# Cross-attention with a routed sign-weight FFN on one core: the gate as stationary operand in four column groups

## The reference

```python
router_logits = n @ gate_w.T                # 1024 tokens x 8 experts
routing = softmax(router_logits)
in_scale = routing @ in_channel_scale       # 1024 x 512
out_scale = routing @ out_channel_scale
out = n * in_scale @ sign(weight).T * out_scale + bias
x = x + out
```

## Time and profile before

| | |
|---|---|
| median of 3 runs | 800.81 us (800.28 to 801.17) |
| the profiled execution | 800.34 us, span 798.5 us |
| TensorE busy | 793.7 us, 99% of the span |
| VectorE, ScalarE, GpSimd busy | 636.6, 359.2, 296.7 us |

### The profile page before, as it was taken

One profiled execution on the slowest core, in us unless ns is written; L12 is line 12 of the kernel. 1 busy time (PEld: TensorE's weight loads), 2 busy tenths in 40 slices (PEclk: granted clock), 3 DMA queues, 4 the chain that ended last, 5 costly groups with the idle time before them and its releaser, 6 DMA issues.

```text
span 798.5 us, 12698 instructions
## 1 busy us (share of the span) xinstructions
PE 793.7 (99%) x4090; PEld 674.9 (85%) x4090; DVE 636.6 (80%) x1066; ACT 359.2 (45%) x949; POOL 296.7 (37%) x279
## 2 busy tenths in 40 slices
PE   9999999999999999999999999999999999999998
PEld 7888888888888888888888888888888888888886
DVE  6877878886893596888888788888888888877775
ACT  6633432432341253545444444444444444447683
POOL 3113021020111032736535544644564454435136
PEclk9999999999999999999999999999999999999999
DMA  8354774584466658627755766575566657553002
GB/s 301 146 196 174 224 247 138 175 266 161 154 191 205 206 166 275 207 65 226 236 163 163 239 191 205 163 240 171 175 210 202 204 157 240 162 196 141 1 1 106
DMA packets 103216, 145.53 MB, mean 182 GB/s; under 512 B 9944, under 2 KB 74584, under 8 KB 97648
## 3 DMA queue, kind: packets, MB, share of 16 engines
q1 hardware_dynamic: 102720, 144.33, 55.5%
q10 hardware_dynamic: 432, 0.39, 0.2%
HBM read 93.31 MB, written 51.38 MB: 181 GB/s over the span
## 4 chain that ended last, share of the span: by engine, by line
PE 98%; DMA 1%; DVE 0%; issue 0%; ACT 0%; SPq 0%; DVEq 0%
PE out L1455 11%; PE out L1457 11%; PE out L1456 11%; PE proj L1457 10%; PE proj L1455 10%; PE proj L1456 10%; PE o L1575 7%; PE s L1549 7%; PE s L1456 4%; PE s L1455 4%; PE s L1457 4%; PE proj L1651 1%; PE t L1603 1%; PE proj L1652 1%; PE t L1559 1%; DMA early<-in_ctx_t 1%
## 5 line engine op out<-in xcount | busy, mean ns | idle before, releaser
L1030 ACT ACTIVATE t<-probs,neg_max 128x128 f32<-128x128 f32 x208 | 74.2, 357 | 112.2 <-DVE neg_max L1295 112.1
L855 POOL TENSOR_TENSOR w_stage<-w_stage 128x256 f32<-128x256 f32 x30 | 24.7, 824 | 264.8 <-DMA w_stage<-in_wk 236.4
L867 POOL TENSOR_TENSOR w_lo<-w_stage,w_hi 128x512 fp32r<-128x512 f32 (+1 forms) x52 | 59.2, 1148 | 134.7 <-ACT w_hi L971 134.7
L1455 PE MATMUL out<-wo_hi,o_hi 128*128 128x512 f32 x224 | 90.6, 405 | 0.1
L1457 PE MATMUL out<-wo_lo,o_hi 128*128 128x512 f32 x224 | 87.8, 392 | 0.0
L1456 PE MATMUL out<-wo_hi,o_lo 128*128 128x512 f32 x224 | 87.4, 390 | 0.0
L1455 PE MATMUL proj<-x_hi,w_hi 128*128 128x512 f32 x210 | 85.0, 405 | 0.0
L1457 PE MATMUL proj<-x_lo,w_hi 128*128 128x512 f32 x210 | 82.4, 392 | 0.0
L1456 PE MATMUL proj<-x_hi,w_lo 128*128 128x512 f32 x210 | 81.8, 390 | 0.0
L879 POOL TENSOR_TENSOR bias_mask<-bias_raw,mask_neg 128x512 f32<-128x512 f32 x64 | 75.7, 1184 | 13.8 <-DVE probs L1292 13.6
L1332 DVE TENSOR_TENSOR acc<-out,acc 128x512 f32<-128x512 f32 x100 | 66.6, 675 | 7.1 <-PE out L1457 7.0
(11 more groups left out here) (362 smaller groups left out, 2100.9 us busy)
## 6 DMA issues: line engine op xcount, KB each, us to landing
k_spill<-ring SPq DMA_DIRECT2D x64, 256.0 KB, 3.4
v_spill<-ring SPq DMA_DIRECT2D x64, 256.0 KB, 2.5
p_turned<-probs SPq DMA_DIRECT2D x208, 64.0 KB, 1.8
probs_t<-p_turned SPq DMA_DIRECT2D x52, 256.0 KB, 4.3
big_stage<-in_wv SPq DMA_DIRECT2D x8, 1024.0 KB, 7.9
w_stage<-in_wq SPq DMA_DIRECT2D x32, 256.0 KB, 3.3
k_first<-k_spill SPq DMA_DIRECT2D x8, 1024.0 KB, 6.0
v_first<-v_spill SPq DMA_DIRECT2D x8, 1024.0 KB, 5.1
```

The lines of the kernel that those rows point to most:

```text
L867: pool.tensor_tensor(lo, staged(m, part), hi.bitcast(F32), ALU.subtract).then_inc(g_wlo, 1)
L1030: last = act.activation(exps_of(j)[:, b], probs[:, j % 2, b, :], ACT.Exp, bias=neg_max[:, col:col + 1], accum_out=row_sum[:, col:col + 1])
L1455: pe.matmul(to[:], left_hi, right_hi, start=first and n == 0, stop=False, skip_group_check=True)
```

## The change

The gate becomes the stationary operand, padded with zeroes from 8 to 32 columns, and the transposed tile the moving one with 128 columns (tokens). Four such products go to the four column groups of 32 of the array (`tile_position`), each with its own 32 partitions of PSUM: groups 0 and 1 hold the first tile's two halves of the features, groups 2 and 3 the second tile's. Two rounds (s) give the four chunks of features. The partial logits, experts on partitions, are copied to SBUF by ScalarE (GC, 128x128), and one small product (GF) with these as stationary operand and a 128x16 matrix of ones and zeroes adds the halves and turns them, into the same `t_bank[:, 0:16]`. GA is gone; G p computes both tiles and waits for both TXC. The matrix is made once by VectorE (GATHER), the gate's padding is zeroed by GpSimd, and the gate's load writes 8 of 32 columns. In the hand-written order, OUT 14 7 moves between G 0 and GF 0, OUT 15 7 to between RT 0 and GF 1, and RT 1 behind OUT 15 6, directly ahead of OS 1. GF 2 stands behind M 1 0, GF 3 behind OS 4.

```diff
+COLS = 32
...
-    steps += [("SCALES",)]
+    steps += [("SCALES",), ("GATHER",)]
...
-              ("TXC", 0), ("BI", 1), ("TXC", 1), ("GA", 0), ("OH", 63), ("NT", 2), ("OL", 63), ("G", 0), ("NT", 3), ("OUT", 15, 4), ("GM", 0),
+              ("TXC", 0), ("BI", 1), ("TXC", 1), ("G", 0), ("OH", 63), ("OUT", 14, 7), ("GC", 0), ("NT", 2), ("OL", 63), ("GF", 0), ("NT", 3),
+              ("OUT", 15, 4), ("GM", 0),
-              ("GA", 1), ("ADD", 15, 5), ("RT", 0), ("BI", 2), ("G", 1), ("ST", 5), ("RTC", 0), ("OUT", 14, 7), ("GM", 1), ("LN2", 2), ("GE", 1),
-              ("ROUTE", 1), ("R", 0, 0), ("OS", 0), ("R", 0, 1), ("Y", 0, 0), ("RT", 1), ("ROOT", 2), ("OUT", 15, 7), ("RTC", 1), ("Y", 0, 1),
-              ("YH", 0, 0), ("LS", 2), ("YH", 0, 1), ("OUT", 15, 6), ("YL", 0), ("OSC", 0), ("YP", 0), ("ADD", 15, 7), ("NT", 4), ("OS", 1),
+              ("G", 1), ("ADD", 15, 5), ("RT", 0), ("BI", 2), ("GC", 1), ("ST", 5), ("RTC", 0), ("OUT", 15, 7), ("GF", 1), ("GM", 1), ("LN2", 2), ("GE", 1),
+              ("ROUTE", 1), ("R", 0, 0), ("OS", 0), ("R", 0, 1), ("Y", 0, 0), ("ROOT", 2), ("Y", 0, 1), ("OUT", 15, 6), ("RT", 1), ("RTC", 1),
+              ("YH", 0, 0), ("LS", 2), ("YH", 0, 1), ("YL", 0), ("OSC", 0), ("YP", 0), ("ADD", 15, 7), ("NT", 4), ("OS", 1),
-              ("TXC", 4), ("BI", 5), ("TX", 5), ("ST", 7), ("YH", 1, 0), ("OS", 2), ("GA", 2), ("TXC", 5), ("LN2", 3), ("Y", 1, 1), ("M", 0, 1),
-              ("ROOT", 3), ("LS", 3), ("YH", 1, 1), ("G", 2), ("YL", 1), ("NT", 6), ("M", 1, 0), ("YP", 1), ("GM", 2), ("MP", 0), ("GE", 2),
+              ("TXC", 4), ("BI", 5), ("TX", 5), ("ST", 7), ("YH", 1, 0), ("OS", 2), ("TXC", 5), ("LN2", 3), ("Y", 1, 1), ("M", 0, 1),
+              ("ROOT", 3), ("LS", 3), ("YH", 1, 1), ("G", 2), ("YL", 1), ("GC", 2), ("NT", 6), ("M", 1, 0), ("YP", 1), ("GF", 2), ("GM", 2), ("MP", 0), ("GE", 2),
-              ("TXC", 7), ("OS", 3), ("BI", 6), ("R", 2, 0), ("R", 2, 1), ("Y", 2, 0), ("GA", 3), ("MP", 1), ("YH", 2, 0), ("SUM", 0),
-              ("M", 2, 1), ("OSC", 3), ("Y", 2, 1), ("G", 3), ("YL", 2), ("YH", 2, 1), ("SUM", 1), ("OS", 4), ("GM", 3), ("M", 3, 0), ("MP", 2),
+              ("TXC", 7), ("OS", 3), ("BI", 6), ("R", 2, 0), ("R", 2, 1), ("Y", 2, 0), ("MP", 1), ("YH", 2, 0), ("SUM", 0),
+              ("M", 2, 1), ("OSC", 3), ("Y", 2, 1), ("G", 3), ("YL", 2), ("GC", 3), ("YH", 2, 1), ("SUM", 1), ("OS", 4), ("GF", 3), ("GM", 3), ("M", 3, 0), ("MP", 2),
...
-        gap = sb("gap", [P, 12 * 256 - 3 * D - B * STACK - DC * E - B * E - 2 * P], F32)
+        gap = sb("gap", [P, 12 * 256 - 3 * D - B * STACK - DC * COLS - B * E - 2 * P - 2 * E], F32)
...
-        gate_sb, exps = sb("gate_sb", [P, DC, E], F32), sb("exps", [P, B, E], F32)
+        gate_sb, exps = sb("gate_sb", [P, DC, COLS], F32), sb("exps", [P, B, E], F32)
+        gather = sb("gather", [P, 2, E], F32)
...
+        part_logits = [probs[:, r, 0] for r in range(2)]
...
-                sp.wait_ge(g_clear, 1)
+                sp.wait_ge(g_clear, 2)
-                sp.dma_start(gate_sb[:], gate_t).then_inc(d_ffn_small, 16)
+                sp.dma_start(gate_sb[:, :, 0:E], gate_t).then_inc(d_ffn_small, 16)
...
+                pool.memset(gate_sb[:], 0.0).then_inc(g_clear, 1)
...
+            def partial_logits(p):
+                act.wait_ge(pe_part, p + 1)
+                if p == 0:
+                    act.wait_ge(pe_t, nth_t["T", len(UNITS) - 1])
+                if p >= 2:
+                    act.wait_ge(pe_gate, p - 1)
+                act.activation(part_logits[p % 2], t_bank[:, 2 * P:3 * P], ACT.Copy).then_inc(a_part, 1)
+
...
+            def gather_matrix():
+
+                dve.wait_ge(pe_prod, max(last_of(n) for n in range(PLAIN, NKV)))
+                units = ident[:].rearrange("p (r k e) -> p r e k", r=2, k=2)[:, :, 0:E]
+                dve.tensor_reduce(gather[:], units, axis=AX.X, op=ALU.add).then_inc(v_gather, 1)
+
...
-                    dve.wait_ge(g_clear, 2)
+                    dve.wait_ge(g_clear, 3)
...
-            def router(p, r):
-                if p == 0 and r == 0:
+            def router(p):
+
+                if p == 0:
-                to = t_bank if r else take(t_bank)
-                pe.wait_ge(a_nt, nth_txc["TXC", 2 * p + r])
-                for c in range(DC):
-                    last = pe.matmul(to[:, r * E:(r + 1) * E], nt_pairs[p][:, r, c * P:(c + 1) * P], gate_sb[:, c, :],
-                                     start=c == 0, stop=c == DC - 1)
-                if r:
-                    last.then_inc(pe_gate, 1)
-                    read_by(to, a_rexp, p + 1)
-
-            def first_router(p):
-                router(p, 0)
-
-            def second_router(p):
-                router(p, 1)
+                to = t_bank if p else take(t_bank)
+                if p:
+                    pe.wait_ge(a_part, p)
+                for r in range(2):
+                    pe.wait_ge(a_nt, nth_txc["TXC", 2 * p + r])
+                for s in range(2):
+                    for group in range(4):
+                        r, c = group // 2, group % 2 * 2 + s
+                        rows = slice(group * COLS, (group + 1) * COLS)
+                        last = pe.matmul(to[rows, 2 * P:3 * P], gate_sb[:, c, :], nt_pairs[p][:, r, c * P:(c + 1) * P],
+                                         start=s == 0, stop=s == 1, tile_position=(0, group * COLS), skip_group_check=True)
+                last.then_inc(pe_part, 1)
+
+            def gather_logits(p):
+                if p == 0:
+                    pe.wait_ge(v_gather, 1)
+                pe.wait_ge(a_part, p + 1)
+                if p:
+                    take(t_bank)
+                pe.matmul(t_bank[:, 0:2 * E], part_logits[p % 2], gather[:].rearrange("p r e -> p (r e)"), start=True,
+                          stop=True).then_inc(pe_gate, 1)
+                read_by(t_bank, a_rexp, p + 1)
...
-                  "PV": probs_times_values, "OUT": output, "TX": ffn_transpose, "GA": first_router, "G": second_router, "RT": transpose_routing,
+                  "PV": probs_times_values, "OUT": output, "TX": ffn_transpose, "G": router, "GF": gather_logits, "RT": transpose_routing,

```

More of the change, by code:

```diff
@@ L510, in xattn_ffn @@
         v_last_res, v_n, v_ones = sem("v_last_res"), sem("v_n"), sem("v_ones")
+        v_gather, pe_part, a_part = sem("v_gather"), sem("pe_part"), sem("a_part")
         v_vsum, v_vs4, v_xsum, v_res = sem("v_vsum"), sem("v_vs4"), sem("v_xsum"), sem("v_res")
@@ L1117, in _ @@
                   "RMSA": rms_roots, "XX": x_high, "EXP": exponentials, "PT": transposed, "OH": out_high,
-                  "WOH": output_weights_high, "SIGN": signs, "SCALES": scales_high, "ROOT": ffn_root, "NT": normal_tile, "TXC": ffn_transposed, "GE": router_exponentials,
+                  "WOH": output_weights_high, "SIGN": signs, "SCALES": scales_high, "ROOT": ffn_root, "NT": normal_tile, "TXC": ffn_transposed, "GC": partial_logits, "GE": router_exponentials,
                   "RTC": routing_transposed, "YH": scaled_high, "OSC": out_scale})
@@ L1432, in _ @@
                   "OL": out_low, "ADD": add_out, "ST": ffn_statistics, "LN2": ffn_norms, "LS": normal_scales, "NT": normal_tile,
-                  "GM": logit_maxima, "ROUTE": route, "Y": scale_tiles, "YL": scaled_low, "MP": scale_product, "SUM": last_sums,
+                  "GATHER": gather_matrix, "GM": logit_maxima, "ROUTE": route, "Y": scale_tiles, "YL": scaled_low, "MP": scale_product, "SUM": last_sums,
                   "MPL": last_scale_product, "SUML": last_sum})
```

## The result

| | before | after |
|---|---|---|
| median | 800.62 us (16 runs, 800.12 to 801.52) | 802.76 us (16 runs, 801.39 to 804.19) |
| ratio to before | | 1.0025 [1.0018, 1.0033] |
| profiled execution, span | 800.34, 798.5 us | 802.05, 800.2 us |
| TensorE busy | 793.7 us | 792.2 us |

What follows compares the result with a forecast made beforehand. TensorE was taken as full only because the order lets other engines just keep up; waits at OS 1 and MP 0 put M 2 0 at +1.74 and GM 3 at +1.78: 800.81 + 1.78 = 802.6 us, range 800.6 to 805.4.

Steps and rivals of the forecast that it cites:

- Step 1 (G 0 waits): At G 0, which now needs both copies of TX 0 and TX 1: it starts 0.37 us later.
- The term G: Cost of one router block of eight products on TensorE: 1.00 us in the middle case, bounded by 0.44 and 1.78.
- steps 2 and 3: From G 0 to pair 1's softmax: GF 1 starts at 765.83 + 2G, GM 1 comes 2.30 us later.
- full-overlap rival: Column groups run side by side, a router block costs 0.44 us: +0.44, median 801.3; chance 0.17.
- switching cost: Rival: entering and leaving column groups waits until the array is empty, +1.0 us on the middle case, 803.6; chance 0.12.
- step 3's formula: Pair 1's softmax: GM 1 starts at 766.22 + 2G, 768.22 at G = 1.00, against 765.92 before.
- step 4: Ahead of OS 1, which needs OSC 0's bank: OS 1 starts 1.55 us later, TensorE stands still about 2.2 us.
- Step 5 (VectorE's row): VectorE from ADD 15 6 to MP 0, read as working without a break: MP 0 and M 2 0 come 1.74 us later.
- Step 6 (pair 3): Pair 3 up to RT 3: nothing on VectorE or ScalarE gets shorter, GM 3 and everything behind come 1.78 us later.
- The clock: Rival: TensorE's pause drops the granted clock to 1.2 GHz, a 4 us stretch costs 4 us more; chance 0.07.
- TensorE's saving: TensorE's own work: 7.2 us of router instructions removed, four pairs at 1.38 (5.5 us) added, 1.7 us less.

Runs made afterwards that it cites:

- e4: After with the router's two loops turned, so that a column group's two products follow each other: 803.32 us (one execution).
- e6: After with all eight products of a router block on column group 0, the other three groups' partial logits left out: 806.04 us (one execution).
- e1: The kernel before, with its own router products, but OUT 14 7, OUT 15 7 and RT 1 placed where the change puts them: 803.80 us.
- e2: After with GF 1 directly behind RT 0, and OUT 15 7 and OUT 15 6 on either side of RT 1: 800.81 us.
- e11: e8 with GpSimd's YP 1 made to wait for NT 6, and MP 0 moved ahead of GM 2 on VectorE: 800.38 us.
- e3: After with eight unused 512-column products on constants behind RT 1, filling TensorE's wait: 801.77 us.
- e5: The kernel before with only the padded gate and its clearing, the gate's load in pieces, and GATHER: 800.97 us.
- e8: e2 with the new tiles in unused SBUF, so that all others keep their addresses of the kernel before: 800.73 us.
- e10: e9 with YL 1 computed by GpSimd instead of VectorE: 800.81 us.
- e9: e8 with ADD 15 7 ahead of YL 0 on VectorE and OSC 3 ahead of YH 2 0 on ScalarE: 800.95 us.

## Why the prediction was right, and where not

Forecast 802.6 us, slower, +1.78; measured 802.76, +2.14. The mechanism, a wait that the order makes ahead of OS 1, was right. That the number is so near is luck: two errors cancel.

1. *Step 1 (G 0 waits):* held; 0.29 us of idle time for the second TXC, and G 0 starts 0.45 us later (759.71 less 758.38 less 0.88), for a forecast of 0.37.
2. *The term G in steps 2 and 3:* mis-sized. Forecast 1.00, measured 0.58 and 0.10 of entry; that is the full-overlap rival, at 0.44, with a switching cost. A block is followed by an instruction at 0.33 instead of 0.23, as before; the last of its four waves is itself followed at 0.2 instead of 0.11. Four waves of 0.11 are the 0.44; entry and exit make it 0.68. So going in and out of the column groups costs about 0.24 us a block; that this is a switch of the engine is argued, not shown. With G = 0.68, step 3's formula gives GM 1 at +1.66 (measured +1.51), step 4's OS 1 at +0.91 (1.55 less 0.64; measured 772.75 less 770.95 less 0.88 = +0.92), the end at +0.92 (0.44 at full overlap and twice 0.24; measured +0.75). The formulas hold; the value put into them failed, because I took matmuls of different groups to go in order. e4 and e6 show that they don't.
3. *Step 4 (OS 1):* held. Forecast some 2.2 us of idle time, measured 2.09, with OSC 0 as releaser; e1 shows it without the new router, e2 takes all but 0.71 us of it away.
4. *Step 5 (VectorE's row):* the delay of MP 0 came (+0.88; 1.74 less 0.64 is +1.10), but the reading was wrong in one place. I called the row from ADD 15 6 to MP 0 unbroken work; 1 us of it was NT 6 waiting for GpSimd (e11). MP 0 hangs on YH 1 1, YP 1 and NT 6, over three engines.
5. *Step 6 (pair 3):* held: what stood at MP 0 (+0.88) is nearly all there at GM 3, +0.75 (785.62 less 783.99 less 0.88). OS 4's own wait of 0.36 us, ahead of GF 3, I had not seen.
6. *The clock:* a rival at 0.07 that came true in ten of sixteen executions, by their mean clock, worth 1.1 us of the 2.14 (e3). I had priced it at 4 us; e4's trace shows 1.5. This error made up for the one in G: at full clock the new order with the new router costs 0.8, the clock 1.1, and the last 0.2 is what e5 shows for the early parts, inside the measurement's uncertainty. The 0.8 is not the order's price by itself: with the old router (e1) the two fastest executions, 802.68 and 802.89 us at mean clocks of 0.999 and 1.000, are still some 2 us above the kernel before, so the shorter blocks give about 1 us of that back.
7. *Where TensorE's saving went:* forecast 1.7 us less work, at G = 1.00; at G = 0.68 the same sum gives 7.2 - 4 x 1.06 = 3.0. The page's busy time falls by 1.5 only, since it counts the end of the record ahead of each gap, which otherwise lies under the next one (RT 1: 0.38 us, where in before the next starts 0.13 later). With the order mended the saving is not won either: from 756 to 795 us the kernel before has no idle time on TensorE, e8 waits some 2 us there (G 0 0.29, OS 1 0.69, TX 6 and M 2 0 0.70, OS 4 0.36), and the ends of the records ahead of these waits come on top. Each of TensorE's gaps has another engine's round trip behind it, which did not get shorter.

## What to carry to other kernels

A round trip is the way of a TensorE result over other engines until TensorE can use it. Where TensorE is full only because its order hides such trips, a cheaper block pays only if the trips get shorter too. So look at what stood between a result and its next user, and do not put an operation directly ahead of the one that needs its round trip. A pause of 2 us on TensorE can cost more than itself, as the clock may fall behind it (1.1 us here). And where a VectorE record is longer than others of its kind and ends together with a GpSimd record or 0.3 us behind it, suspect a wait, and test it by ordering the two with a semaphore.

## What the runs showed of the hardware that was not expected

- Eight plain fp32 products, each with 32 stationary and 128 moving columns, take 0.58 us on four column groups where one group takes 1.87 (after, e6); with the loops turned it is 0.60 (e4).
- Loads of weights are not taken ahead at the borders of such a block: after's row of weight loads shows 0.36 us of idle time put down to "issue" at the blocks of pairs 1, 2 and 3 (0.46 at pair 0), and 0.20 behind those of pairs 0, 1 and 2. Pair 2's:

```profile
776.59 0.38 PEld L1630 LDWEIGHTS t<-k_first,gate_sb 128*32 128x32 f32 x16 [0.36 <-issue]
777.17 0.19 PEld L1680 LDWEIGHTS proj<-x_hi 128*128 128x128 f32 x1 [0.20 <-issue]
```

- Pauses of 2.09 us (e1, e4) and 2.02 us (e5) were followed by a fall of the granted clock (0.73 over 5 us, 0.50 over 2 us, 0.64 over 4 us), those of 2.09 us in after and e6 were not. With 0.71 us the profiled execution of e2 stays at 1.00, and the mean of its eleven is 0.999 or 1.000.
- Some of VectorE's operations with all operands in SBUF do not end before the GpSimd instruction beside them does: 1.52 against 0.54 us for the same 128x512 one (e8, e11), 0.53 against 0.16 and 0.84 against 0.25 for ones of two columns (e10, e9). Others are not held: the statistics of `acc` (BATCH_NORM_STATS2) that start at 771.88 in before take 0.69 us, as elsewhere, with GpSimd busy from 771.11 to 773.65.
